# Vector and scalar engine steps that wait on their own counter in place of a drain after every step

## The reference

```
xn   = layernorm(x)
qkv  = quant(xn) @ wqkv.T          # quant: round to 8 bits by the row's largest value
q, k = rope(q), rope(k)            # 16 query heads, 4 key/value heads, 128 each
o    = causal_softmax(q k^T / sqrt(128)) v
s    = quant(rmsnorm(o) * norm_w) @ wo.T
h    = silu(quant(xn) @ tern(w_gate).T) * (quant(xn) @ tern(w_up).T)     # 8192 wide
f    = quant(rmsnorm(h) * ln_weight) @ tern(w_down).T                    # tern: round to -1, 0, 1
out  = x + s * silu(f)
```

## Time and profile before

| what | value |
|---|---|
| median of 6 runs | 10218.12 us (10204.33 to 10268.85) |
| the profiled execution, its time | 10268.85 us |
| its span on the slowest core (core 3) | 10267.3 us |
| spans of the eight cores | 10227.6 to 10267.3 us |
| busy on core 3: PE, DVE, ACT | 4611.7, 3610.5, 755.4 us (45%, 35%, 7%) |
| chain that ended last, by engine | PE 38%, DVE 25%, DMA 22%, issue 7%, ACT 4%, DVEq 3% |

### The profile page before, as it was taken

How to read it: one execution, slowest core, us unless ns; L and a number is a source line. 1 busy time by engine, 2 the same in 40 slices (tenths; PEclk the granted TensorE clock), 3 DMA queues, 4 the chain that set the end, 5 groups by cost and what they waited for, 6 DMA issues and landing times.

```text
span 10267.3 us, 68808 instructions; the slowest of 8 cores (10227.6 to 10267.3 us)
## 1 busy us (share of the span) xinstructions
PE 4611.7 (45%) x19950; PEld 2023.4 (20%) x19950; DVE 3610.5 (35%) x5305; ACT 755.4 (7%) x722; POOL 164.9 (2%) x258
## 2 busy tenths in 40 slices
PE   0000000001244454544547862878457882868637
PEld 0000000000011111322323321333223331323213
DVE  4675665666433324232221016000440006110260
ACT  0000000000000001213230010000100001000100
POOL 0000000000000000000000000000000000000000
PEclk9999999999967675766768985988668895878758
DMA  5776776761100011220203330433214330343304
GB/s 199 231 233 239 226 221 240 215 186 37 53 17 17 22 28 34 48 45 7 45 4 99 115 99 1 152 120 105 66 50 148 115 114 18 106 129 110 98 9 148
DMA packets 561861, 1064.36 MB, mean 104 GB/s; under 512 B 17363, under 2 KB 472019, under 8 KB 506067
## 3 DMA queue, kind: packets, MB, share of 16 engines
q1 hardware_dynamic: 478836, 866.48, 27.1%
q0 software_dynamic: 82656, 193.48, 6.8%
HBM read 963.94 MB, written 144.70 MB: 108 GB/s over the span
## 4 chain that ended last, share of the span: by engine, by line
PE 38%; DVE 25%; DMA 22%; issue 7%; ACT 4%; DVEq 3%; SPq 1%; ACTq 0%; POOLq 0%; POOL 0%
PE quad L882 9%; PE quad L1026 9%; PE quad L874 9%; DMA ab<-tg 6%; PE quad L553 5%; ACT ab L665 3%; DMA td<-ab 3%; DMA tu<-ab 2%; DMA tg<-ab 2%; DVE ab L992 2%; DVE ab L385 2%; DVE wacc L342 2%; PE quad L657 2%; DMA af<-wdT 2%; DMA af<-wgT 2%
## 5 line engine op out<-in xcount | busy, mean ns | idle before, releaser
L874 PE MATMUL quad<-ab 128*128 128x512 bf16 x4096 | 1116.6, 431 | 630.8 <-DMA ab<-tg 630.8
L899 DVE SCALAR_TENSOR_TENSOR ab<-quad,c_au,ab 128x512 bf16<-128x512 f32 x256 | 192.2, 751 | 2306.5 <-PE quad L882 2306.5
L882 PE MATMUL quad<-ab 128*128 128x512 bf16 x4096 | 964.6, 390 | 0.0
L1026 PE MATMUL quad<-ab 128*128 128x512 bf16 x4096 | 900.4, 384 | 3.4 <-DVEq L126 3.4
L348 PE MATMUL quad<-onescol,wtot 128*1 128x1 f32 x6 | 0.6, 163 | 1729.2 <-DVEq L126 1729.2
L874 PEld LDWEIGHTS quad<-ab 128*128 128x128 bf16 x4096 | 426.1, 106 | 1265.7 <-issue 911.3
L553 PE MATMUL quad<-ab 128*128 128x512 bf16 x1536 | 524.5, 518 | 161.3 <-DMA ab<-wqkvT 161.3
L342 DVE TENSOR_REDUCE wacc<-af 128x1 f32<-128x2048 f32 x192 | 438.9, 2286 | 411.6 <-DMA af<-wdT 138.3
L882 PEld LDWEIGHTS quad<-ab 128*128 128x128 bf16 x4096 | 414.3, 101 | 530.2 <-issue 106.8
L989 PE MATMUL tra<-identb,ab 128*128 128x128 bf16 x512 | 135.9, 265 | 818.3 <-DVEq L126 818.3
L1026 PEld LDWEIGHTS quad<-ab 128*128 128x128 bf16 x4096 | 404.2, 99 | 498.5 <-issue 43.1
(11 more groups left out here) (172 smaller groups left out, 3932.4 us busy)
## 6 DMA issues: line engine op xcount, KB each, us to landing
af<-wgT SPq DMA_DIRECT2D x128, 1024.0 KB, 6.3
af<-wuT SPq DMA_DIRECT2D x128, 1024.0 KB, 6.3
af<-wdT SPq DMA_DIRECT2D x128, 1024.0 KB, 6.4
ab<-tg SPq DMA_DIRECT2D x128, 1024.0 KB, 8.5
ab<-tu SPq DMA_DIRECT2D x128, 1024.0 KB, 10.7
ab<-td SPq DMA_DIRECT2D x64, 2048.0 KB, 8.4
tg<-ab POOLq DMA_DIRECT2D x64, 512.0 KB, 7.1
tu<-ab POOLq DMA_DIRECT2D x64, 512.0 KB, 7.5
```

The costliest lines, as they stand in the source:

```text
L874: tg_mm = p.do("tensor", lambda e, f=f, ti=ti, gi=gi: e.matmul(quad_ap(gi), AB.ap(qxq_off + f * 512 + ti * 128, 128), AB.ap(wg_off + f * 5 ...
L882: tu_mm = p.do("tensor", lambda e, f=f, ti=ti, ui=ui: e.matmul(quad_ap(ui), AB.ap(qxq_off + f * 512 + ti * 128, 128), AB.ap(wu_off + f * 5 ...
L899: e.scalar_tensor_tensor(AB.ap(hq_off + ti * DI + ob * 512, 512), quad_ap(ui), st_au.ap()[:, tt:tt + 1], sg, ALU.mult, ALU.mult),
L1026: "tensor", lambda e, f=f, ti=ti, fg=fg, buf=buf: e.matmul(quad_ap(ti), AB.ap(hq_off + ti * DI + fg * 128, 128), AB.ap(buf + f * 512, 512) ...
```

## The change

`do` gives every DVE and ACT step a count of its own semaphore. `emit` no longer writes a drain and a no-op behind each of them, but only behind those recorded with `drain=True`; a plain step carries the increment itself, as PE's matmuls do. And in front of every DVE and ACT step, behind its other waits, stands a new wait, for the count that the step before it on the same engine will set.

```diff
@@ def do
-        if inc:
+        auto = eng in ("vector", "scalar")
+        if inc or auto:
             sem = SEM_OF[eng]
             self.cnt[sem] += 1
             tok = (sem, self.cnt[sem])
@@ def emit
-            auto_drain = eng_name in ("vector", "scalar")
+            chain = eng_name in ("vector", "scalar")
+            own = SEM_OF.get(eng_name)
 
             def body(e):
+                prev = 0
                 for (fn, waits, tok, drain, incn) in self.ops[eng_name]:
                     for (sem, val) in waits:
                         e.wait_ge(sems[sem], val)
+                    if chain and prev > 0:
+                        e.wait_ge(sems[own], prev)
                     inst = fn(e)
                     if tok is not None:
-                        if drain or auto_drain:
+                        if drain:
                             e.drain()
                             e.nop().then_inc(sems[tok[0]], incn)
                         else:
                             inst.then_inc(sems[tok[0]], incn)
-                    elif drain or auto_drain:
+                        if chain:
+                            prev = tok[1]
+                    elif drain:
                         e.drain()
             return body
```

## The result

The changed kernel takes 10143.57 us (median of 17 runs, 10119.60 to 10243.66), the kernel before 10224.93 beside it (38 runs, 10190.17 to 10327.63). The ratio is 0.9916, 95% interval 0.9898 to 0.9933. On the median of 10218 that is 86 us less (68 to 104), where 89 were summed. The profiled execution took 10202.95 us, 59 above the median.

The account below looks back on a forecast made before the run. No engine is full; chains of steps and the gaps between them bound the kernel. Terms -2 + 1 - 44 + 22 - 7 - 57 - 2 = -89 us, from the median 10218 to about 10130 us; range 10055 to 10220.

Parts of the forecast that it names:

- The two prices: On DVE and ACT: a step behind a drained one gains a wait, +0.066 us; behind a plain one, -0.075 us.
- g: Gap behind a plain step, from attached increment through released wait to next step's start: taken as 0.10 us, 0.175 before.
- w: Cost of one satisfied semaphore wait in an engine's queue: 0.066 us.
- Rival A: DVE's queue in QKV and norms: own attached increment returns late, from 0.15 us; 10379 us at 0.24; chance 0.10.
- Rival B: Engine's own flush fills the gap, waits free: 10218 us (hard); softer, gap 0.12 to 0.175: 10165 to 10265; chance 0.15.
- rival C: Half the waits behind drained steps free, 10078 us, or plain gap 0.066, 10068; both 10016; chance 0.17.
- The copies' round: Transposes' copies in the norms: copy, PE's transpose and wait through one tile, 0.80 us for two copies, -0.07 a copy.
- the norms of `h`: 16 tiles: 15 waits +0.99, copies and plain gaps outweigh them, -3.54 us a tile, -57 us.
- the norm of `x`: 16 tiles: waits behind drained steps against plain gaps and copies, +0.05 us a tile, +1 us; the two prices cancel.
- Attention: Heads: 224 waits at exponentials and masks +15, evicting steps +4 and +3, nothing in the last two query blocks: +22 us.
- The cover that was counted for gate and up: Waits before L894 and L899 put at nothing behind 16 matmuls of the next bank; without that cover +34 us.
- QKV: 80 tiles with rope: DVE's chain counts in full, -0.54 us a tile, -44 us, PE's clock taken as before.

Follow-up runs that it names:

- X1: Changed kernel, but every DVE and ACT step keeps drain and no-op and also gets the wait: 10520.54 us, 1.0257 of the kernel before.
- X2: Changed kernel with the new wait only behind plain steps, none behind drained ones: 10037.10 us, 0.9790 of the kernel before.
- X5: Kernel before with the change in the whole QKV stage only: 10159.32 us in one run, 10247.02 for the kernel before.
- X6: Kernel before with the change only in rope's scaling and first products in QKV: 10208.63 us in one run, 10247.02 for the kernel before.
- X4: Changed kernel without ACT's waits on its own counter: 10142.16 us in its one run.
- X3: Changed kernel with no drain at all; every DVE and ACT step carries its increment and waits: 9966.35 us, 0.9729 of the kernel before.
- X8: Changed kernel without the own wait in front of the copies behind the transposes: 10052.03 us in one run.
- X7: As X3, and 13 recorded steps that don't depend on the step in front go without the wait: 9805.97 us, 0.9562 of the kernel before.

## Why the prediction was right, and where not

The forecast of 10130 us was right: on its base the measured ratio gives 10132 (10114 to 10150). The two prices held as well. Where the gain came from didn't: two misses of stages offset each other, as told below.

- The two prices. g was put at 0.10 and is 0.106 to 0.109; w at 0.066, and the waits on DVE take 0.064 to 0.069. X1 and X2 measure each price by itself, and the ratios expected, 1.027 and 0.981 to 0.983, lie within the measured intervals. Rival A needed g above 0.15. Rival B's hard form is excluded by X1, its soft form by the gap of 0.106. The Trainium skill (VectorE: DVE Perf Modes, section "The DRAIN you can't avoid") has semaphores between vector steps cost nothing; X1's ratio of 1.0257 disagrees with it. Of rival C, which gave 10016 to 10078, both conditions fail.
- The copies' round was the largest term with a reckoned mechanism: 0.80 a pair forecast, 0.81 in the rows and 0.825 on the mean; the norms of `h` -57 forecast, -51 measured against the one execution of before and -45 against X5 and X6. The 0.025 a pair make 512 x 0.025 = 13 us, about the difference.
- The two prices cancel in the norm of `x` (+1 forecast and measured), and X1 and X2 show both halves: +44 with waits and no gain, -22 with gain and no waits.
- Attention was under-sized: +22 forecast, +33 and +35 measured. By query block it is +7, +8, +8 and +10 (+12 in the second execution), where 6, 6, 4 and 5 were counted, so most of the miss lies in the last two. The evicting steps show two causes. The first query block of the changed kernel shows the small one:

```profile
3822.93 0.59 PE L692 MATMUL pva<-ab 128*128 128x129 bf16 x4 [4.12 <-DVEq L131]
...
3823.70 0.17 DVE L700 RECIPROCAL o_inv<-pva 128x1 f32<-128x1 f32 x1 [1.10 <-PE pva L692]
3824.11 0.35 DVE L703 TENSOR_SCALAR ab<-pva,o_inv 128x128 bf16<-128x128 f32 x1 [0.24 <-DVEq L131]
...
3824.68 0.59 PE L692 MATMUL pva<-ab 128*128 128x129 bf16 x4 [0.72 <-DVEq L131]
3824.76 0.17 DVE L700 RECIPROCAL o_inv<-pvb 128x1 f32<-128x1 f32 x1 [0.30 <-DVEq L131]
...
3825.74 0.59 PE L692 MATMUL pvb<-ab 128*128 128x129 bf16 x4 [0.47 <-DVEq L131]
```

PE now waits 0.72 us for its tile where it waited 0.60, and then 0.47 where it waited 0.34. Reciprocal and scaling each gained a wait: gaps of 0.30 and 0.24 behind a drain, 0.24 and 0.18 before. Over all heads this makes 0.32 a head, where 4 x 0.066 = 0.26 was counted: one us in all. The other cause is the third query block, costed at nothing because a longer chain on PE was to cover the eviction. Before, then after:

```profile
4564.10 1.51 PE L685 MATMUL pvb<-ab 128*128 128x129 bf16 x12
...
4564.76 0.35 DVE L696 TENSOR_SCALAR ab<-pva,o_inv 128x128 bf16<-128x128 f32 x1 [0.18 <-issue]
...
4565.40 1.51 PE L685 MATMUL pva<-ab 128*128 128x129 bf16 x12
```

```profile
4498.19 1.50 PE L692 MATMUL pvb<-ab 128*128 128x129 bf16 x12
...
4498.98 0.35 DVE L703 TENSOR_SCALAR ab<-pva,o_inv 128x128 bf16<-128x128 f32 x1 [0.24 <-DVEq L131]
...
4499.55 0.70 PE L692 MATMUL pva<-ab 128*128 128x129 bf16 x5
```

The scaling, which frees `pva`, starts 0.66 us behind the chain into `pvb` before and 0.79 after, two waits later; PE's next chain starts 1.30 and 1.36 behind it. So of the 0.13 only 0.07 were covered. On the mean of all heads PE's step into the third and the fourth chain of a head (from the start of the last matmul in front) rose there from 0.13 and 0.12 to 0.22 and 0.36 us, and the block by 7.8 us where its exponentials and masks give 16 x (3 + 1) x 0.066 = 4.2. In the fourth block these steps stayed within 0.03 us, and what made it 4 to 7 us longer than counted I can't say. The cover that was counted for gate and up did hold: -2 and +3 us there.
- QKV is the term that was wrong in size: -44 forecast, -91 and -94 measured. The chain gave -0.54 a tile, as summed. The step that failed is the sentence that took PE's clock "as granted before": it rose from 0.71 to 0.77, and the 16 matmuls of a tile took 4.91 us where they took 5.45. That is 80 x 0.54 = 43 us more, as much again as the chain, and it is shown for QKV's own change by X5.
- That the total still came out so near is luck. QKV gave 47 to 50 us more than forecast. The norms and the heads, by the stages of X5 and X6, gave 8 us where 41 were summed, 33 less: 14 in the heads, 12 in the norms of `h`, the rest in the other two norms. The weights can't be read to 20 us. X5's time says the same: QKV alone makes 88 us, the whole change 86. Both rest on single executions or runs, so the split is good to some 20 us and its direction is clear.

What stays open is what sets the clock in QKV. The table has, for every run but X4 (as the changed kernel), the chain from a tile's last matmul to its last transpose, the granted clock of the stretch, and the 16 matmuls of a tile:

| | X1 | before | X6 | X5 | after | X2 | X3 | X8 | X7 |
|---|---|---|---|---|---|---|---|---|---|
| chain, us | 7.05 | 6.41 | 6.14 | 5.86 | 5.86 | 5.77 | 5.77 | 5.58 | 5.13 |
| clock (median core) | 0.68 | 0.70 | 0.73 | 0.76 | 0.76 | 0.78 | 0.77 | 0.79 | 0.75 |
| 16 matmuls, us | 5.40 | 5.45 | 5.23 | 4.95 | 4.91 | 4.75 | 4.81 | 4.70 | 5.06 |

From before to X8 a shorter chain goes with a higher clock and faster matmuls. At both ends it doesn't: X1 has a longer chain than before and its matmuls are no slower, and X7 has the shortest chain and slower matmuls than X8. That the clock's gain belongs to the change in QKV is shown by X5; that the length of the chain is what it answers to is not. No run here tells why.

## What to carry to other kernels

A semaphore wait that is always satisfied isn't free in a chain of short steps: here each costs 0.066 us, and in the norm of `x` one ahead of every step ate all that the dropped drains saved; attach the increment to the step, drop the drain, and wait only where a step depends on the one in front (X7, 4.4% off). Price a wait by where it stands in the queue: behind a late wait it still adds (the exponential started 0.15 us behind its last matmul with it and 0.11 without). Where a cost is put at nothing because another engine covers it, work the margin out from rows; in the third query block 0.07 us were there and 0.13 were needed. And check a total by its stages: this one was right while QKV was off by 47 to 50 us and the norms and heads by 33 the other way.

## What was not expected of the hardware

- A step of DVE can start before the step in front of it has ended, if no wait stands between: the gap of L389 in X7 is 0.0 for 192 steps, and rope's first two products, in order of time, start 0.34 us apart there at 0.42 to 0.43 us each:

```profile
2689.52 0.43 DVE L588 TENSOR_TENSOR af<-af,ropec 128x256 f32<-128x256 f32 x1
2689.86 0.42 DVE L590 TENSOR_TENSOR af<-af,ropes 128x256 f32<-128x256 f32 x1
```

- In the form with drain and no-op, the no-op is the larger part of the 0.175 us: from its start to that of the step behind it pass 0.104 to 0.109 us (2002 places on core 3 before). A satisfied wait takes 0.064 to 0.069.
- PE's granted clock in QKV rose when the chain on DVE got shorter, from 0.70 to 0.76, and gave as much again as the chain (43 us each), yet was lower, 0.75, with the shortest chain.
- One die's cores can lose 60 us in a single stage of a single execution (down, 960 against 898 us), with the granted clock at 0.81 for 350 us; this level is in the traces besides 1.2 and 2.4 GHz.
